# Three reorderings in a hand-ordered slot-attention step: denominators before the root's spread, their reciprocal before the scores, the new gate's sum before the exponentials' inverse

## The reference, cut to what matters

```python
sn = rmsnorm(slots, slot_norm_w)
q_proj = sn @ Wq.T
scores = jnp.einsum('bkd,bmd->bkm', q_proj, k_proj) * SCALE
attn = jax.nn.softmax(scores, axis=-2)                      # over the 128 slots
attn = attn / (jnp.sum(attn, axis=-1, keepdims=True) + EPS) # over the 77 context rows
updates = jnp.einsum('bkm,bmd->bkd', attn, v_proj)
slots = gru_cell(updates, slots, gru_wih, gru_whh, gru_bih, gru_bhh)
```

## Time and profile before

| | |
|---|---|
| median of 3 runs | 1630.61 us (1629.01 to 1631.13) |
| the profiled execution's own time | 1634.47 us |
| its span in the trace | 1632.6 us |
| mean granted clock of PE | 0.942 |
| PE busy | 1443.6 us (88%) |
| DVE busy | 1272.2 us (78%) |
| POOL busy | 1252.6 us (77%) |
| ACT busy | 1096.3 us (67%) |
| slot stage, first hn matmul to the last step's | 941.74 to 1394.31 us from the span's start |

### The profile page before, as it was taken

How to read it: one execution, slowest core, us unless ns; L and a number is a source line. 1 busy time by engine, 2 the same in 40 slices (tenths; PEclk the granted TensorE clock), 3 DMA queues, 4 the chain that set the end, 5 groups by cost and what they waited for, 6 DMA issues and landing times. The chain is left out here.

```text
span 1632.6 us, 22044 instructions
## 1 busy us (share of the span) xinstructions
PE 1443.6 (88%) x6146; PEld 876.3 (54%) x6146; DVE 1272.2 (78%) x2207; ACT 1096.3 (67%) x2118; POOL 1252.6 (77%) x861
## 2 busy tenths in 40 slices
PE   4889999999999989998998699999999999529994
PEld 1333343434343434343333377778777787429993
DVE  1999999999999999999999257777777777714552
ACT  4778877887788778887786366666666666204552
POOL 1899999999999999999999334477777766434665
PEclk8999999999999999999999799999999999759997
DMA  5455455545554555455543353303418000036771
GB/s 170 147 182 177 164 183 184 176 158 180 181 178 161 178 183 180 160 187 188 175 151 124 90 190 129 138 30 135 152 42 327 14 8 12 11 111 193 210 206 38
DMA packets 126058, 236.92 MB, mean 145 GB/s; under 512 B 13490, under 2 KB 76917, under 8 KB 125952
## 3 DMA queue, kind: packets, MB, share of 16 engines
q1 hardware_dynamic: 121408, 227.21, 42.4%
q0 software_dynamic: 4544, 8.47, 1.5%
HBM read 180.89 MB, written 55.66 MB: 145 GB/s over the span
## 5 line engine op out<-in xcount | busy, mean ns | idle before, releaser
L388 POOL TENSOR_TENSOR hc<-state,c_rows 128x1024 f32<-128x1024 f32 x256 | 598.7, 2359 | 49.9 <-DVE state L585 40.3
L585 DVE TENSOR_TENSOR_SCAN state<-ps_da,inp 128x512 f32<-128x512 f32 x512 | 593.2, 1205 | 29.5 <-ACT ps_da L481 29.5
L704 PE MATMUL ps_y<-hc,ident 128*128 128x512 f32 x1024 | 495.1, 623 | 55.4 <-POOL hc L388 55.3
L481 ACT ACTIVATE ps_da<-dt,a_neg 128x512 f32<-128x512 f32 x512 | 345.1, 688 | 81.6 <-DVE state L585 79.1
L704 PEld LDWEIGHTS ps_y<-hc,ident 128*128 128x128 f32 x1024 | 195.6, 198 | 298.7 <-issue 214.9
L574 DVE TENSOR_TENSOR inp<-dtx,ps_b 128x1024 f32<-128x1024 f32 x192 | 230.7, 1202 | 39.2 <-POOL dtx L359 22.9
L1063 POOL TENSOR_TENSOR rs<-ms,m_half 128x4 f32<-128x4 f32 x48 | 59.2, 1232 | 136.2 <-DVE ms L1250 136.0
L371 POOL TENSOR_TENSOR inp<-dtx,b_rows 128x1024 f32<-128x1024 f32 x64 | 150.8, 2356 | 0.1
L627 PE MATMUL ps_misc<-x1T,w_conv 128*128 128x512 f32 (+3 forms) x256 | 118.4, 607 | 21.5 <-ACT x1T L414 21.5
L1180 ACT ACTIVATE ex<-sc,nmx,ctx_r 77x128 f32<-77x128 f32 x192 | 92.4, 482 | 64.9 <-DVE nmx L1263 64.9
L487 ACT COPY ps_b<-b_rows 128x512 f32<-128x512 f32 x192 | 111.1, 579 | 36.6 <-DVE inp L574 35.1
(11 more groups left out here) (234 smaller groups left out, 2731.5 us busy)
## 6 DMA issues: line engine op xcount, KB each, us to landing
b_rows<-bc_rows SPq DMA_DIRECT2D x128, 512.0 KB, 4.6
c_rows<-bc_rows SPq DMA_DIRECT2D x128, 512.0 KB, 3.9
sorted_x<-pad_rows SPq DMA_DIRECT2D x8, 4160.0 KB, 16.0
w<-in_L_ffn_W SPq DMA_DIRECT2D x78, 256.0 KB
vw<-vw_rows SPq DMA_DIRECT2D x16, 462.0 KB
vw_rows<-vw_out SPq DMA_DIRECT2D x16, 384.0 KB
xrow<-sorted_x SPq DMA_DIRECT2D x39, 130.0 KB, 2.3
x_tok<-in_x SPq DMA_DIRECT2D x16, 256.0 KB, 3.8
```

Of the source, the lines that this page charges most:

```text
L388: pool.tensor_tensor(hc[:, n % RING], state[:, n % RING], over_c(c_rows[:, slot, n % 2]), ALU.mult).then_inc(hc_ready, 1)
L481: act.activation(ps_da[u % DA_RING][:], dt[:, par, c], ACT.Exp, scale=a_neg[:, c, n:n + 1]).then_inc(da_ready, 1)
L585: dve.tensor_tensor_scan(state[:, n % RING, c], ps_da[u % DA_RING][:], inp[:, n % RING, c], 0.0, ALU.mult, ALU.add).then_inc(state_ready, 1)
L704: ins = pe.matmul(ps_y[:, c], ident[:], hc[:, n % RING, c], start=False, stop=n == NS - 1)
```

## The change

It moves three calls and alters nothing else; no instruction is added or removed, and every wait stays on the instruction that has it.

```diff
--- before.py
+++ after.py
@@ -1421,10 +1421,10 @@
             g = post(n, 0)
             if g is not None and g >= END:
                 end_residual(g)
+            if live(n - 1):
+                denominators(n - 1)
             if live(n):
                 maxima(n)
-            if live(n - 1):
-                denominators(n - 1)
             if live(n - 2):
                 reset(n - 2)
             if live(n - 1):
@@ -1445,10 +1445,10 @@
             if g is not None and n >= N:
                 statistics(g)
                 end_veps(g)
+            if live(n - 2):
+                new_in(n - 2)
             if live(n):
                 normaliser(n)
-            if live(n - 2):
-                new_in(n - 2)
 
     @blk.tensor
     def _(pe):
@@ -1558,10 +1558,10 @@
             g = post(n, 5)
             if g is not None:
                 count(g)
+            if live(n - 1):
+                den(n - 1)
             if live(n):
                 root_spread(n)
-            if live(n - 1):
-                den(n - 1)
             if live(n - 2):
                 gate_h(n - 2, 1, ps_z, z_read)
             if live(n - 1):
```

## The result

The changed kernel is slower: 1652.51 us median (1651.34 to 1656.55, 4 runs) against 1630.84 (1629.01 to 1631.13, 4 runs), a ratio of 1.014, 95% interval 1.0121 to 1.0158. The prediction, 1630.8 with a range of 1623.5 to 1636.5, is too low by 22 us. The profiled execution has a span of 1650.4 us, 17.8 more than before. By the first matmul of gate_hn, the 45 full steps take 460.7 us (937.94 to 1398.63) where they took 437.0 (941.74 to 1378.74): +23.7; the rest, -5.9, lies in the stage's start (1.1 shorter, from the first sum of squares to that matmul), in its last two steps (0.1) and outside the stage.

The account below looks back on a forecast made before the run. The prediction took PE's pace plus its waits as the bound, mainly den_spread's wait for the reciprocal; +8.3 (plain steps), -7.4 (make_u steps) and -0.7 (start) gave +0.2, so 1630.8 us, range 1623.5 to 1636.5.

Parts of the forecast that it names:

- The wait moves from den_spread to the sums of squares: PE in plain steps: the 0.45 us wait before den_spread disappears; PE waits about 0.5 us before ssq instead.
- Plain step 9.44, +0.25 x 33: The 33 full steps without make_u: 9.44 us each in place of 9.19, +8.3 us in all.
- The restart: PE from the products' end to the start of scores, through ssq: 1.02 us, bounds 0.86 to 1.09.
- rival A: PE restarts at ssq free of charge: plain step 9.28, total 1625.5 us; chance 0.24.
- make_u steps 9.64, -7.4: The 12 steps with make_u, whose work covers PE's wait: 9.64 us in place of 10.26, -7.4 in all.
- new_in at nothing: DVE's move of new_in before normaliser: costs nothing, since rse and rser are needed 4 us and more later.
- Start -0.7: First steps, where PE has few gates: spread earlier, root_spread later, -0.7 us (0 to -1.3).
- End 0: Step 47, without ssq: PE wins 0.45 us, but DVE releases the next den_spread anyway, so 0.
- Rival B: POOL's half slows DVE's rh by 0.38 us in the 33 plain steps: +12.5, 1643.3 us; chance 0.12.
- Rival C: Nothing moves: an input holds den until root_spread could have gone, 1630.6 us; chance 0.04.

Follow-up runs that it names:

- e5: Changed kernel plus an extra 256-column matmul pair before the sums of squares, except in make_u steps: 1636.28 us, ratio 1.0031.
- e10: Kernel before with only new_in moved ahead of normaliser on DVE: 1633.3 us, ratio 1.0008.
- e8: Kernel before with only den moved ahead of root_spread on PE: 1669.89 us, ratio 1.0232.
- e3: Kernel before with only the reciprocal moved ahead of the scores' maxima on DVE: 1657.68 us, ratio 1.0159.
- e11: Changed kernel with den as 128-column matmuls, sums of squares still one column wide: 1654.84 us, ratio 1.0146.
- e2: Changed kernel with scores(n + 1) ahead of ssq(n + 1) on PE: 1612.81 us, ratio 0.9888.
- e6: Changed kernel with the sums of squares as 128-column matmuls in place of one-column ones: 1635.99 us, ratio 1.0026.
- e12: Changed kernel with scores ahead of ssq, POOL's scatter split over two steps, and 128-column sums of squares: 1607.65 us, ratio 0.9857.
- e1: Changed kernel plus an extra 256-column matmul pair before every sum of squares: 1639.87 us, ratio 1.0044.

## Why the prediction was wrong

- **The wait moves from den_spread to the sums of squares**: right, 33 times, with 0.52 idle and the products at 4.90.
- **Plain step 9.44, +0.25 x 33**: right while the clock stands, 9.46. The restart was 1.03 (0.15 + 0.88; I took 1.02, with 0.86 to 1.09 as ends), rival A with its 0.86 is refuted. With count's and the first rounds' steps at +0.3, the term measures +9.8 in e5 (5.1 + 4.7) in place of +8.3.
- **make_u steps 9.64, -7.4**: right where POOL's root is in time. In six (of e5) it is not, even behind den, and by e5 the twelve sum to about 119 us against 123.7 before: -4.7. I had let den hide the whole lateness, and had no row of POOL beside it.
- **The step that failed** is one that the prediction never wrote as a term: every duration was taken at a clock of 1.00, because the earlier trace rows showed 1.00, and the clock was carried over to an order that puts half a microsecond of idleness beside 0.81 us of one-column matmuls. It cost 18.6 of the 23.7 us in the steps: 13 stretches at 1.2 GHz, where the prediction had none. The start of the stage at half the clock was in my rows, and I used it as a price list for a restart, not as a warning. No rival was about the clock, and the range held nothing for it.
- **new_in at nothing**: right (e10). **Start -0.7**: the stretch to the first gate is 1.1 shorter. **End 0**: the last two steps sum to 15.5 for 15.6.
- **Rival B**, POOL on rh: rh is 0.68 to 0.69 in the loop and 0.66 before, never 1.04. The 1.5 us that the prediction puts down to its citation there is the length of half in the earlier trace rows; what it cites gives a rule and no figure.
- **Rival C** did not occur.

The Trainium skill (TensorE: Matmul & The Clock Gate, A second HAM failure mode: psum-queue depth-cycling) says that small pauses between groups of matmuls, if frequent, can make PE's clock swing between its levels. The trace of the changed kernel agrees, with 13 falls in 45 steps. The runs add what kind of pause did it here: 1.1 us a step between wide matmuls did not (e8), half a microsecond in front of one-column matmuls did (the changed kernel, e3, e11), and ten waits behind such matmuls did not (e2).

## What to carry to other kernels

A wait is not priced by its length alone: ask what stands beside it on PE. The one-column sums are busy in the trace, and half a microsecond of waiting in front of them still went with falls of the clock; the same wait in front of 128-column sums did not. So make such a block wider where the width is as good as free, as it was here (0.04 us a step in e6, nothing in e12), or fill the wait with the step's next real work, which here turned a loss of 22 us into a gain of 19 (e2, 1612.81 us against 1632.23 for the kernel before in its rounds). And when a loop sits at full clock, write the clock down as a term of its own before moving idle time about in it.

## What the runs showed of the hardware that was not expected

- Eight fp32 passes of one column took 0.81 us from their start to that of the next block, eight of 128 columns 0.87 to 0.89 (e6, e11, e12): the columns are all but free there.
- Half a microsecond of waiting in front of one-column sums brought 12 to 14 falls of the clock in the 45 steps (changed kernel 13, e3 14, e11 12). Filling it with a 0.43 us pair (e1, e5) or widening the sums (e6) left none. Each fall lasted about 3.4 us and cost about 1.5 us.
- Ten waits of 0.48 to 0.92 us directly behind the one-column den brought no fall (e2). Whether the side of the wait decides, or chance among ten, was not tested.
- Why only 13 of the changed kernel's 33 waits are followed by a fall was not settled; the runs show where falls begin, not what decides between two like steps.
